# A two-layer graph network on one core: third and fourth y product exchange banks, gate rows and turned attention go through DRAM

## The reference

```
# layer 0
Q = x @ W_q + b_q;  K = x @ W_k + b_k;  V = x @ W_v + b_v      # 8 heads of 64
a = x @ w_g[:D];    c = x @ w_g[D:]
s = Q K^T / 8 + a[:, :, None] + c[:, None, :] + b_g + log(adj + 1e-9)
x1 = softmax(s) @ V + x
# layer 1
s1 = (x1 Wq + bq) (x1 Wk + bk)^T / sqrt(512), masked where adj == 0
ctx = (softmax(s1), 0 where adj == 0) @ x1 @ Wc
out = layernorm(x1 + ctx) * gamma + beta
```

## Time and profile before

| | us |
|---|---|
| median of 3 runs (lowest, highest) | 2406.81 (2406.55, 2409.76) |
| the profiled execution | 2408.92 |
| its span, first to last instruction | 2407.1 |
| TensorE busy | 2321.3 |
| VectorE busy | 1754.0 |
| ScalarE busy | 1219.3 |
| GpSimd busy | 894.4 |

### The profile page before, as it was taken

One profiled execution on the slowest core, in us unless ns is written; L12 is line 12 of the kernel. 1 busy time (PEld: TensorE's weight loads), 2 busy tenths in 40 slices (PEclk: granted clock), 3 DMA queues, 4 the chain that ended last, 5 costly groups with the idle time before them and its releaser, 6 DMA issues.

```text
span 2407.1 us, 39433 instructions
## 1 busy us (share of the span) xinstructions
PE 2321.3 (96%) x13520; PEld 1898.1 (79%) x13520; DVE 1754.0 (73%) x5476; ACT 1219.3 (51%) x3474; POOL 894.4 (37%) x1146
## 2 busy tenths in 40 slices
PE   7999999999999999999999999999999999999985
PEld 5778888788888788888788887788887888887774
DVE  4667777777777677777777776777776777776766
ACT  4454455555455544445544455544545554555442
POOL 0243334443334433334433344432344433344423
PEclk9999999999999999999999999999999999999997
DMA  6223333323333323333323333233333233333221
GB/s 233 93 88 110 105 101 115 119 84 103 113 106 106 118 93 96 111 114 106 107 96 101 102 127 106 91 107 106 102 118 115 84 106 110 105 110 115 75 70 45
DMA packets 155768, 253.26 MB, mean 105 GB/s; under 512 B 17072, under 2 KB 99120, under 8 KB 151344
## 3 DMA queue, kind: packets, MB, share of 16 engines
q1 hardware_dynamic: 155568, 250.75, 32.2%
HBM read 150.02 MB, written 100.66 MB: 104 GB/s over the span
## 4 chain that ended last, share of the span: by engine, by line
PE 95%; DVE 3%; ACT 1%; SPq 1%; DMA 0%; issue 0%; POOL 0%; DVEq 0%
PE bank L206 27%; PE bank L208 25%; PE bank L207 25%; PE bank L437 6%; PE bank L450 5%; PE bank L473 5%; DVE y_lo L1061 1%; ACT y_hi L748 1%; PE bank L367 1%; PE bank L482 1%; PE bank L421 1%; DVE x1n L1000 0%; DMA x1n<-in_wkT 0%; DVE bnst L1070 0%; DVE x1n L1067 0%
## 5 line engine op out<-in xcount | busy, mean ns | idle before, releaser
L1204 POOL TENSOR_TENSOR probs<-probs,rcp 128x512 f32<-128x512 f32 x256 | 261.2, 1040 | 1294.7 <-DVE rcp L942 1294.7
L714 ACT ACTIVATE probs<-probs,nmax 128x128 f32<-128x128 f32 x1024 | 397.3, 391 | 196.4 <-DVE nmax L932 196.4
L1000 DVE STREAM_TRANSPOSE x1n<-x1T 32x512 f32<-32x512 f32 x512 | 359.9, 703 | 116.9 <-DMA out<-x1n 109.8
L206 PE MATMUL bank<-x_hi,wk_hi 128*128 128x512 f32 x512 | 209.9, 410 | 50.0 <-DVE y_lo L1061 42.3
L735 ACT ACTIVATE g_sb<-bank,consts 128x512 f32<-128x512 f32 x128 | 88.0, 688 | 316.5 <-PE bank L208 314.7
L932 DVE CUSTOM_DVE_ANT_0 probs<-bank,bias 128x128 f32<-128x128 f32 x1024 | 227.6, 287 | 1.5 <-issue 0.2
L703 ACT ACTIVATE q_sb<-bank,consts 128x512 f32<-128x512 f32 x128 | 88.0, 688 | 274.3 <-PE bank L208 274.3
L1212 POOL TENSOR_TENSOR x_lo<-xT_land,x_hi 128x512 fp32r<-128x512 f32 x124 | 169.5, 1396 | 148.8 <-ACT x_hi L668 148.8
L206 PE MATMUL bank<-x_hi,wm_hi 128*128 128x512 f32 x512 | 206.0, 402 | 9.7 <-DVE x_lo L964 9.7
L951 DVE STREAM_TRANSPOSE turned<-probs 128x1024 f32<-128x1024 f32 x128 | 158.7, 1240 | 71.5 <-POOL probs L1204 67.3
L206 PE MATMUL bank<-x_hi,wq_hi 128*128 128x512 f32 x512 | 208.7, 408 | 0.0
(11 more groups left out here) (128 smaller groups left out, 5339.8 us busy)
## 6 DMA issues: line engine op xcount, KB each, us to landing
turn_dram<-turned SPq DMA_DIRECT2D x128, 512.0 KB, 2.6
probsT<-turn_dram SPq DMA_DIRECT2D x512, 128.0 KB, 2.8
out<-x1n SPq DMA_DIRECT2D x128, 256.0 KB, 3.2
xn<-in_x SPq DMA_DIRECT2D x126, 256.0 KB, 2.7
xT_land<-in_xT SPq DMA_DIRECT2D x31, 1024.0 KB, 6.4
adj_sb<-in_adj SPq DMA_DIRECT2D x32, 256.0 KB, 3.3
v_sb<-in_wk SPq DMA_DIRECT2D x4, 256.0 KB, 5.4
xT_land<-in_xT SPq DMA_DIRECT2D x4, 256.0 KB, 5.6
```

The source lines that it names most:

```text
L206: nc.tensor.matmul(out_ap, st[0], mv[0], start=start, stop=False)
L714: op = nc.scalar.activation(probs[:, k, :], probs[:, k, :], ACT.Exp, bias=nmax[:, k:k + 1], scale=-1.0, accum_out=sums[:, k:k + 1])
L1000: op = nc.vector.transpose(x1n[b * BLK:(b + 1) * BLK, :, :] .rearrange("p g (c a s) -> p a c g s", c=C, a=P // BLK)[:, a, :, :, :], x1T[a ...
L1204: nc.gpsimd.tensor_tensor(probs[:, half, :], probs[:, half, :], rcp[:, half].unsqueeze(2).to_broadcast([P, HALF, P]), ALU.mult)\
```

## The change

`y_bank` gives the y products 2 and 3 of a step the banks 1 and 0 instead of 0 and 1, and the waits follow: K projection 0 waits for y 2, Q projection 0 for y 3.

`gate_rows` is gone. SP's new `spread_c` stores c (128 x 4) to DRAM, waits, and loads it back as one row of 512 into all 128 partitions of a new tile c_rows. `bias` reads c_rows, each graph's values four elements apart, instead of bank 7.

`turn_attention` leaves TensorE in all steps but the last. On VectorE a new function of that name turns att1 in 32x32 blocks into scratch, right behind `attention1`; SP's new `move_attention` stores scratch to DRAM, waits, and loads it back in four pieces into c_rows. `att1T_high` and `att1T_low` read c_rows instead of bank 7. On ScalarE `att1T_high` now stands behind the eviction of Q 3, not ahead of it. The gate sums wait for the stores that still read scratch or c.

```diff
         def y_bank(g, last):
-            return bank[((4, 5, 2, 3) if last else (2, 3, 0, 1))[g]]
+            return bank[((4, 5, 2, 3) if last else (2, 3, 1, 0))[g]]
...
+            def spread_c(t):
+
+                sp.wait_ge(s["dve_a"], nth("dve_a", t, 3))
+                sp.dma_start(c_dram, c_c[:, :]).then_inc(s_cst0, 16)
+                sp.wait_ge(s_cst0, 16 * (t + 1))
+                if t > 0:
+                    sp.wait_ge(s["dve_b"], nth("dve_b", t - 1))
+                if t > 1:
+                    sp.wait_ge(s["dve_tp"], nth("dve_tp", t - 2))
+                sp.dma_start(c_rows[:, :], c_dram.rearrange("(o j) g -> o (j g)", o=1).to_broadcast([P, P * GG]))\
+                    .then_inc(s_crow, 16)
+
+            def move_attention(u):
+
+                sp.wait_ge(s["dve_at"], nth("dve_at", u))
+                sp.dma_start(at_dram, scratch[:, :]).then_inc(s_as, 16)
+                sp.wait_ge(s_as, 16 * (u + 1))
+                for b in range(P // BLK):
+                    sp.dma_start(c_rows[b * BLK:(b + 1) * BLK, :].rearrange("r (a x) -> r a x", a=P // BLK),
+                                 at_dram.rearrange("(a r) (b x) -> b r a x", a=P // BLK, b=P // BLK)[b])\
+                        .then_inc(s_al, 16)
...
                 if w >= 0:
-                    pe.wait_ge(s["dve_y"], nth("dve_y", w, 3))
+                    pe.wait_ge(s["dve_y"], nth("dve_y", w, 2))
...
                 project_k(t, 0)
                 if w >= 0:
                     context_rest(w)
-                    pe.wait_ge(s["dve_tp"], nth("dve_tp", w))
-                else:
-                    pe.wait_ge(s_lo["m"], 4)
-                gate_rows(t)
-                if w >= 0:
-                    pe.wait_ge(s["dve_y"], nth("dve_y", w, 2))
+                if w >= 0:
+                    pe.wait_ge(s["dve_y"], nth("dve_y", w, 3))
...
-                pe.wait_ge(s["dve_sa"], nth("dve_sa", u))
-                turn_attention(u, False)
                 project_q(t, 3)
...
                 k_out(t, 3)
+                q_out(t, 3)
                 att1T_high(u, False)
-                q_out(t, 3)
...
-                dve.wait_ge(s["pe_cb"], nth("pe_cb", t))
+                dve.wait_ge(s_crow, 16 * (t + 1))
                 dve.wait_ge(s["act_ln"], nth("act_ln", t))
+                c_row = c_rows[:, :].rearrange("p (j g) -> p g j", g=GG)
                 for g in range(GG):
-                    op = nc.vector.scalar_tensor_tensor(out=bias0[:, g, :], in0=bank[7][:, g * P:(g + 1) * P],
+                    op = nc.vector.scalar_tensor_tensor(out=bias0[:, g, :], in0=c_row[:, g, :],
                                                         scalar=a_c[:, g:g + 1], in1=ln_adj[:, g, :],
...
+            def turn_attention(u):
+                dve.wait_ge(s["dve_att1"], nth("dve_att1", u))
+                nc.vector.transpose(scratch[:, :].rearrange("p (b g s) -> p b g s", b=P // BLK, g=GG),
+                                    att1[:, :, :].rearrange("p g (b r) -> p b g r", b=P // BLK))\
+                  .then_inc(s["dve_at"], 1)
...
                 attention1(u)
+                turn_attention(u)
                 maxima(t, 2)
```

More of the change, by code:

```diff
@@ L149, in gnn_program @@
         s_pw = [sem(f"turned_stored{c}") for c in range(C)]
+        s_cst0 = sem("c_stored")
+        s_crow = sem("c_rows_loaded")
+        c_dram = nc.dram_tensor("c_dram", (P, GG), f32, kind="Internal").ap()
+        s_as = sem("att_turned_stored")
+        s_al = sem("attT_loaded")
+        at_dram = nc.dram_tensor("at_dram", (P, GG * P), f32, kind="Internal").ap()
         PT_MOVES = P // BLK
@@ L181, in y_bank, with att_land @@
         def y_bank(g, last):
-            return bank[((4, 5, 2, 3) if last else (2, 3, 0, 1))[g]]
+            return bank[((4, 5, 2, 3) if last else (2, 3, 1, 0))[g]]
         def y_split(g, last):
             return (x_hi[:, g, :], x_lo[:, g, :]) if last else (y_hi[g % 2][:, :], y_lo[g % 2][:, :])
-        def tp_bank(last):
-            return bank[1 if last else 7]
+        def att_land(order):
+            return c_rows[:, :].rearrange(f"p (a g s) -> {order}", a=P // BLK, g=GG)
         def ctx_bank(g, last):
@@ L415, in project_v @@
                 hi_lo(bank[2 + g % 2][:, :], act_rows(x_hi, x_lo, g), w_rows("v")).then_inc(s["pe_v"], 1)
[L417 to L423, removed]
             def scores(t, c):
@@ L476, in pair_scores @@
                 mm.then_inc(s["pe_sa"], 1)
-            def turn_attention(u, last):
+            def turn_attention(u):
                 pe.wait_ge(s["dve_att1"], nth("dve_att1", u))
                 for g in range(GG):
-                    mm = nc.tensor.transpose(tp_bank(last)[:, g * P:(g + 1) * P], att1[:, g, :], ident[:, :])
+                    mm = nc.tensor.transpose(bank[1][:, g * P:(g + 1) * P], att1[:, g, :], ident[:, :])
                 mm.then_inc(s["pe_tp"], 1)
@@ L751, in att1T_high @@
             def att1T_high(u, last):
-                act.wait_ge(s["pe_tp"], nth("pe_tp", u))
-                nc.scalar.activation(flat(att1T_hi), tp_bank(last)[:, :], ACT.Copy).then_inc(s["act_tp"], 1)
+                if last:
+                    act.wait_ge(s["pe_tp"], 1)
+                    nc.scalar.activation(flat(att1T_hi), bank[1][:, :], ACT.Copy).then_inc(s["act_tp"], 1)
+                    return
+                act.wait_ge(s_al, 16 * PT_MOVES * (u + 1))
+                nc.scalar.activation(att1T_hi[:, :, :].rearrange("p g (a s) -> p g a s", a=P // BLK),
+                                     att_land("p g a s"), ACT.Copy).then_inc(s["act_tp"], 1)
             def next_x_high(it):
@@ L969, in gate @@
                     dve.wait_ge(s["dve_a"], nth("dve_a", t, g - 1))
+                    if g == 2 and t > 1:
+                        dve.wait_ge(s_as, 16 * (t - 1))
                 elif t > 0:
                     dve.wait_ge(s["dve_a"], nth("dve_a", t - 1, GG - 1))
+                    dve.wait_ge(s_cst0, 16 * t)
                 nc.vector.tensor_tensor_reduce(out=scratch[:, :], in0=rows, in1=wg1_b[:, :],
@@ L1054, in att1T_low, with turn_attention @@
                 dve.wait_ge(s["act_tp"], nth("act_tp", u))
-                nc.vector.tensor_tensor(flat(att1T_lo), tp_bank(last)[:, :], flat(att1T_hi).bitcast(f32),
-                                        ALU.subtract).then_inc(s["dve_tp"], 1)
+                if last:
+                    nc.vector.tensor_tensor(flat(att1T_lo), bank[1][:, :], flat(att1T_hi).bitcast(f32),
+                                            ALU.subtract).then_inc(s["dve_tp"], 1)
+                    return
+                in_blocks = "p g (a s) -> p g a s"
+                nc.vector.tensor_tensor(att1T_lo[:, :, :].rearrange(in_blocks, a=P // BLK),
+                                        att_land("p g a s"),
+                                        att1T_hi[:, :, :].rearrange(in_blocks, a=P // BLK).bitcast(f32),
+                                        ALU.subtract).then_inc(s["dve_tp"], 1)
+            def turn_attention(u):
+                dve.wait_ge(s["dve_att1"], nth("dve_att1", u))
+                nc.vector.transpose(scratch[:, :].rearrange("p (b g s) -> p b g s", b=P // BLK, g=GG),
+                                    att1[:, :, :].rearrange("p g (b r) -> p b g r", b=P // BLK))\
+                  .then_inc(s["dve_at"], 1)
             def y_low(u, g, last):
```

27 lines of the change are left out of this document (16 added, 11 removed).

## The result

The changed kernel takes 2368.86 us (median of 4 runs, 2368.32 to 2369.99) against 2407.35 us (2406.55 to 2409.76) before: a ratio of 0.984, 95% interval 0.982 to 0.986. The forecast was 2365.5 us. The profiled execution of the changed kernel has a span of 2368.2 us, 38.9 us under that of the earlier trace rows.

A forecast was written before the change was run, and what follows sets the result against it. TensorE, busy 96% of the span, was taken as the bound: 2407.1 - 81.8 (swap and transposes) + 39 (bias) + 1.5 (start) = 2365.8 us of span, forecast 2365.5 us; range 2322 to 2385 us.

The forecast's parts named there:

- The swap: Turn of a step: exchanging banks 0 and 1 removes TensorE's wait for y's low half, gain 51.6 us.
- The covers: Spare time before K and Q projections need y's banks: 1.0 us for K, 2.5 us for Q.
- The transposes: TensorE without attention and gate-row transposes: 0.50 and 0.46 us each time, gain 30.2 us.
- The attention's way: Turn, store and loads take some 6.8 us; cover 2.2 us; low half and context product meet within 0.1 us.
- Gate rows through DRAM: c's store and broadcast take about 6.2 us; the bias asks after 9.6 us, cover 3.4 us.
- The bias's new source: VectorE's bias alternates with GpSimd's gamma and beta products, delaying the residual sum: TensorE stalls 1.3 us per step, 39 us.
- the shift of 0.3 us: At the turn of the step, VectorE's work comes some 0.3 us later, an estimate.
- The first rival: VectorE gets both gaps between GpSimd's products: bias stall 0.35 us, 2337 us; chance 14%.
- the second: Rival: the bias does not collide with GpSimd's products, 2326.5 us; chance 15%.
- The start: First step: c's store stands behind the loads of the start, costing 1.5 us (0 to 4).
- The third rival: The attention lands late, each us beyond the cover costing 31 us; with a late broadcast of c, 10% together.

The follow-up runs named there:

- the mended kernel: Changed kernel with the residual sum of graph 3 ahead of the bias and the gate rows of step 0 on TensorE: 2327.48 us.
- two stores more: Changed kernel with the turned attention stored three times in sequence, each waited for, ahead of its loads: 2379.88 us.
- with three: Changed kernel with the turned attention stored four times in sequence, each waited for, ahead of its loads: 2482.82 us.
- that one exchange of two lines: Changed kernel with the residual sum of graph 3 ahead of the bias on VectorE: 2334.69 us.

## Why the prediction was right

The forecast of 2365.5 us missed by 3.4 (0.5 of them in the median before, 2407.35 with a fourth run, where the prediction had 2406.81). By its own steps:

**The swap**, 51.6 us: 52.4 measured alone. The covers held: K and Q projection never waited for y. K's was 0.5 us in the changed kernel, half of what was worked out.

**The transposes**, 30.2 us: 12.8 for the attention (15.5 worked out), and 15.7 for the gate rows, the difference between the mended kernel and the one with gate rows on TensorE (14.3 worked out for 31 steps). Together 28.5. Step by step both terms held: 0.49 us for 0.50, and for the gate rows 70.61 - 70.14 = 0.47 for 0.46. What the attention's total lacks lies at the start, which has a spread of its own.

**The attention's way.** Its mechanism held, down to the even meeting of low half and context product. The cover was under-sized: 4 us, not 2.2, since I took store and loads from the probabilities' (2.7 and 2.8 us), twice as large; they took 2.0 and 1.9. The block turn took 0.71, not 0.65. The other 0.5 us of the cover are ScalarE's: it asked 10.2 us behind the attention (1221.20 - 1211.03), where 9.65 were worked out.

**Gate rows through DRAM.** 5.9 us from the store's issue (1.4 and 4.5) against the 6.2 of the working, by two errors in opposite directions: the store of 2 KB is quicker than the bound, the broadcast slower than beta's. The cover held.

**The bias's new source**, the step that turned the sum: right in place, kind and order of turns. 39 us were forecast, 32.7 are there as waits and 34.2 came back when they were removed. Mis-sized was the shift of 0.3 us: the bias starts 8.30 us behind the last y matmul, before it started 8.19 behind it, so 0.1. VectorE's work did shift, and by more: y product 2's low half starts 0.95 us ahead of the last y matmul, where it started 1.46 ahead, so 0.5. But most of this ended there, for y product 3's low half had waited 0.29 us for ScalarE's high half and could come later by as much. Its row in the kernel before, in VectorE's order of time:

```profile
1247.02 0.69 DVE L1061 TENSOR_TENSOR y_lo<-bank,y_hi 128x512 fp32r<-128x512 f32 x1 [0.29 <-ACT y_hi L748]
```

Beta's product followed gamma's after 0.07 us instead of 0.15, and the operations behind it took 0.80 us to the residual sum instead of 0.66; these two cancel in part. The first rival (both gaps for VectorE) and the second (no collision) are refuted by the four single rows.

**The start**, 1.5 us forecast with 4 at most: 7.4 by the trace, 7.2 by experiment. This is the term that failed. The store of c needed 5.2 us among the loads of the start and the broadcast 4.9, 10.1 where 6.2 to 8 were taken; that made the bias 4.5 us late. The rest was not in the working at all: behind the longer wait TensorE ran a second stretch at the lower granted clock, which only the kernels with c's first trip through DRAM show. That error and the smaller wait of each step, 1.1 for 1.3 us, nearly cancel, so the total looks better than its parts.

**The third rival** did not come, but its price was wrong. Each us beyond the cover was to cost 31 us. With two stores more that holds (12.0 us of waits, 11.0 us of time); with three, 71 us of waits cost 114, because the clock fell behind 26 of the 31.

## What to carry to other kernels

When an operand is moved from PSUM to SBUF to relieve TensorE, look at what it makes of the reader: a VectorE operation that now has two SBUF inputs stands beside a GpSimd instruction for its whole length, and whatever is queued behind it is late too. Put the operation that the bound engine waits for ahead of it; here that one exchange of two lines was worth 34 us, as much as most of the change. And price a stall on TensorE by its length and by what it can do to the clock behind it, which the stall's length alone did not tell here; a term that is paid once, at the start, needs the rows of the start, not those of the steps.

## What the runs showed of the hardware

Reading SBUF at every fourth element in place of PSUM cost a 128x128 bias operation 0.09 us: 1.48 against 1.11 us for four, with GpSimd idle or at its short operations.

Behind one wait of 1.86 us TensorE ran at 0.53 of its clock for 3.5 us (8 matmuls, 0.43 for 0.23 us); behind another of 1.86 us, and behind one of 2.46 us in another run, it kept the full clock. Behind waits of 1.08 and 1.41 us no fall is in the rows.

A DMA store of 2 KB to DRAM landed in 1.4 us, one of 256 KB in 2.0, one of 512 KB in 2.6; a broadcast of one 2 KB row into 128 partitions took 4.5 us in the steps, where the same form, beta's load, had taken 3.2 once in the kernel before.
